# A fused two-layer kernel: the second read of sorted rows in two pieces, and four recurrences moved into later expert slots

## The chip, the cores and the metric

One core of a Trainium2 chip (trn2). The metric is the device time in microseconds, from the launch's start on the device to its end; lower is better. Engines are called by their names or as the profile does: TensorE (PE, its weight loads PEld), VectorE (DVE), ScalarE (ACT), GpSimd (POOL), SyncE (SP).

## The reference, cut to what matters

Eight sequences of 512 tokens with 128 features pass two layers, in float32. Each layer computes `x = x + s * silu(moe(xn))` with `xn = layernorm(x)`. In layer 0, `s` is a gated linear recurrence; in layer 1 it is causal linear attention.

```python
# layer 0, s: per sequence and feature, a scan over the 512 tokens
x_scan = sigmoid(xn @ Wg.T + bg) * tanh(xn @ Wv.T + bv)
a = 0.001 + 0.998 * sigmoid(xn @ Wd.T + bd)
h[t] = a[t] * h[t-1] + x_scan[t]
# layer 0, moe: 4 groups of 2 experts, the best group of a token, both its experts
out = sum_e w[e] * (silu(xn @ gate_w[e]) * (xn @ up_w[e])) @ down_w[e]
```

## The kernel before, in words

**Routing and sorting.** The 32 tiles of 128 tokens are split in two parts of 12 and 20 tiles (`PT`). VectorE computes for each token the row (slot) that it gets in an order sorted by expert group. GpSimd then writes each tile's normalised rows (128 features and 2 expert weights, 520 bytes) to `sorted_rows` in DRAM with one indirect DMA a tile (`scatter`, L422, 32 in all). SyncE reads the sorted rows back (L350 to L352): when part 0's 12 scatters have landed, tiles 0 to 8 (`FULL` = 9 tiles, which part 0 alone fills), and when part 1's 20 have landed, tiles 9 to 34. `sorted_in[h]` counts each read.

**Expert slots.** Layer 0's experts run in `SORTED` = 35 slots, one sorted tile in each. In slot n TensorE (`late_slot`, L934) runs three gate matmuls (L901 to L903), turns the rows of tile n+1 (L926), runs three up matmuls, the eight down matmuls of tile n-2 (L921) and four transposes of the hidden values of tile n-1 (L931). Between them ScalarE does SiLU (L621), the rounding copy of the next rows (`sxT_out`, L616), the copy of the turned hidden values (L625) and of the result (L630). VectorE does the remainder of the next rows (`rest_of_rows`, L1407), without which the next gate can't start, and the product gate x up (L1417). TensorE waits at slot 8 (`FULL - 1`) for `sorted_in[1]`, since slot 8 turns tile 9.

**Recurrences.** Sequence q goes through `rec_project` (three matmuls of 512 columns, L842), `rec_tanh` on ScalarE (decay L564, gate L566, content L567, scaling of the decay L570), `rec_value` (L1336) and `rec_scan` (L1343) on VectorE, `rec_turn` (four transposes, L850) on TensorE and `rec_out` (L575) on ScalarE. The engines' orders are written out by hand and are in-order queues joined by semaphores. Sequences 0 to 4 are scanned before the slots; `LATE` = 3 sequences (5 to 7) have value and scan in slots 0 to 5 and are turned in slots 2, 4, 6 (`TURN_AFTER`). `rec_turn(4)` stands between the up matmuls of slot 0 and the turn of tile 1. All four activations of sequence 7 stand ahead of slot 0's SiLU. Its projection is in banks 3 to 5 of PSUM; gate and up use banks 0 to 3, the turned hidden values bank 4, the down product bank 6, rows bank 7.

**Weights.** Layer 0's expert weights are split in a rounded part (ScalarE, L580) and a remainder (`w_rest`, VectorE, L1349), four groups. Two copies on VectorE (L1401, L1402) hold a fused weight; TensorE waits for them (`fused_out`) before it turns tile 0. After the last `rec_turn` GpSimd splits the layer 1 weights (`split_w13` and others, L438 to L459), since a part of them lies where `scan` lay, and then gathers results (L432) once the first 16 tiles' results are stored.

## Time and profile before

| | |
|---|---|
| median of 3 runs | 391.16 us (390.8 to 391.41) |
| profiled execution | 389.67 us, its span 387.5 us |
| mean granted TensorE clock | 0.982 of 2.4 GHz |
| busy share of the span | TensorE 95%, VectorE 71%, ScalarE 60%, GpSimd 59% |
| chain that ended last | TensorE 77%, ScalarE 8%, GpSimd 4%, DMA 4%, VectorE 4% |
| TensorE's longest wait | 5.2 us, for the read of the sorted rows |

The span runs from the first to the last instruction; the execution's own time has the launch around it as well. A busy share is a mean over very different stages, so the slots are read from the views by time. A line of the timeline is: start, duration, engine, source line, operation, what is written and read, the count, and in brackets how long the engine stood idle before and who ended that.

### The profile page before, as it was taken

The numbers are of one execution on the slowest core, as the hardware profiler recorded it, in microseconds if no ns is written. First come the engines' busy times: TensorE is split into PE (matmuls) and PEld (weight loads), VectorE is DVE, ScalarE is ACT, GpSimd is POOL, SyncE is SP. The second block draws the span as 40 slices with busy tenths as digits, with TensorE's granted clock in tenths as the row PEclk, the third lists the DMA queues.
The fourth block names the chain that finished last, engine by engine and source line by source line (L and its number), as shares of the span: only waits on it lengthen the run. The fifth ranks groups of instructions, "written<-read, shape, count | busy, mean of one in ns | idle before, by whom it ended". The sixth has DMA issues, their size and how long they took to land.

```text
span 387.5 us, 6422 instructions
## 1 busy us (share of the span) xinstructions
PE 368.6 (95%) x1904; PEld 288.7 (74%) x1904; DVE 275.0 (71%) x769; ACT 231.5 (60%) x462; POOL 227.9 (59%) x215
## 2 busy tenths in 40 slices
PE   6999879949999999999999999999999999999996
PEld 5785348938888988876778778778778777786784
DVE  5989957613343547538869889889799799787663
ACT  3777975515545574769675584785675755932312
POOL 4537887690005218207966967977968869267461
PEclk9968999989999999999999999999999999999999
DMA  7997311340013001054240250340600601405100
GB/s 228 270 346 286 92 58 47 108 107 2 0 41 99 28 2 29 0 184 164 69 179 0 68 207 0 112 162 3 255 17 22 253 0 44 203 3 194 51 29 27
DMA packets 26592, 38.66 MB, mean 100 GB/s; under 512 B 2496, under 2 KB 22848, under 8 KB 24128
## 3 DMA queue, kind: packets, MB, share of 16 engines
q1 hardware_dynamic: 24512, 34.03, 26.5%
q0 software_dynamic: 2048, 4.23, 3.4%
q8 instruction: 17, 0.28, 0.3%
q14 instruction: 15, 0.12, 0.1%
HBM read 29.20 MB, written 9.05 MB: 99 GB/s over the span
## 4 chain that ended last, share of the span: by engine, by line
PE 77%; ACT 8%; POOL 4%; DMA 4%; DVE 4%; issue 3%; ACTq 0%; DVEq 0%
PE ps L1072 9%; PE ps L1040 8%; PE ps L1038 8%; PE ps L1039 8%; PE ps L921 6%; PE ps L901 4%; PE ps L842 3%; PE ps L903 3%; PE ps L902 3%; PE ps L1019 3%; PE ps L931 3%; POOL sorted_rows L422 3%; PE ps L990 2%; DMA sorted_sb<-sorted_rows 2%; PE ps L1055 2%
## 5 line engine op out<-in xcount | busy, mean ns | idle before, releaser
L484 POOL TENSOR_TENSOR gu<-gu 128x512 f32<-128x512 f32 x64 | 87.7, 1372 | 52.3 <-DVE gu L1575 48.3
L1038 PE MATMUL ps<-xc_round,w_round 128*128 128x512 f32 (+1 forms) x145 | 74.9, 517 | 0.6 <-DVE gu L1550 0.5
L706 ACT ACTIVATE gu<-gu 128x512 f32<-128x512 f32 x64 | 40.3, 630 | 56.9 <-DVE gu L1575 55.9
L1040 PE MATMUL ps<-xc_round,w_rest 128*128 128x512 f32 (+1 forms) x145 | 57.1, 394 | 0.0
L1039 PE MATMUL ps<-xc_rest,w_round 128*128 128x512 f32 (+1 forms) x145 | 56.7, 391 | 0.0
L432 POOL DMA_INDIRECT xnT<-sorted_y,slot x32 | 31.7, 990 | 38.6 <-DMA sorted_y<-sorted_sb 32.2
L1575 DVE TENSOR_TENSOR gu<-ps,w_raw 128x512 f32<-128x512 f32 x64 | 43.6, 686 | 11.7 <-PE ps L1040 9.7
L1407 DVE TENSOR_TENSOR sx_rest<-ps,sx_round 128x128 fp32r<-128x128 f32 x35 | 10.2, 291 | 57.6 <-ACT sx_round L616 57.6
L625 ACT COPY h0T<-ps 128x512 f32<-128x512 f32 x35 | 20.5, 587 | 43.7 <-PE ps L931 43.7
L1072 PE MATMUL ps<-gu,w2s 128*128 128x512 f32 x90 | 46.0, 593 | 0.0
L422 POOL DMA_INDIRECT sorted_rows<-sorted_sb,slot x32 | 36.2, 1130 | 14.8 <-issue 9.4
L901 PE MATMUL ps<-w_round,sx_round 128*128 x70 | 34.5, 493 | 7.8 <-DMA sorted_sb<-sorted_rows 5.2
L921 PEld LDWEIGHTS ps<-w0d,h0T 128*128 128x128 f32 x280 | 37.2, 193 | 3.2
L921 PE MATMUL ps<-w0d,h0T 128*128 x280 | 37.3, 276 | 0.0
L1038 PEld LDWEIGHTS ps<-xc_round,w_round 128*128 128x128 f32 x145 | 27.4, 189 | 11.7 <-issue 7.6
L1039 PEld LDWEIGHTS ps<-xc_rest,w_round 128*128 128x128 f32 x145 | 27.5, 190 | 10.2 <-issue 7.7
L1417 DVE SCALAR_TENSOR_TENSOR h<-sg,sorted_sb,ps 128x256 f32<-128x256 f32 x70 | 30.2, 473 | 3.3 <-PE ps L931 2.6
L1040 PEld LDWEIGHTS ps<-xc_round,w_rest 128*128 128x128 f32 x145 | 27.2, 188 | 6.1
L903 PE MATMUL ps<-w_rest,sx_round 128*128 x70 | 28.1, 402 | 0.0
L902 PE MATMUL ps<-w_round,sx_rest 128*128 x70 | 28.1, 401 | 0.0
L1575 DVE TENSOR_TENSOR gu<-ps,w0d 128x512 f32<-128x512 f32 x32 | 21.6, 683 | 7.6 <-PE ps L1040 7.5
L621 ACT ACTIVATE sg<-ps 128x512 f32<-128x512 f32 x35 | 21.0, 599 | 10.0 <-PE ps L903 10.0
(230 smaller groups left out, 831.2 us busy)
## 6 DMA issues: line engine op xcount, KB each, us to landing
w_raw<-score_rows SPq DMA_DIRECT2D x8, 1024.0 KB, 5.9
spread_first<-score_rows SPq DMA_DIRECT2D x4, 1024.0 KB, 4.9
w0d<-score_rows SPq DMA_DIRECT2D x4, 1024.0 KB, 7.1
sorted_rows<-zero_rows SPq DMA_DIRECT2D x1, 2340.0 KB, 15.7
xa<-in_x SPq DMA_DIRECT2D x8, 256.0 KB, 4.5
w_raw<-in_gate_up SPq DMA_DIRECT2D x1, 2048.0 KB, 13.9
out_x<-xa SPq DMA_DIRECT2D x7, 256.0 KB, 2.2
sorted_sb<-sorted_rows SPq DMA_DIRECT2D x1, 1690.0 KB, 9.0
```

What stands on the lines that cost most here:

```text
L422: pool.indirect_dma_start(sorted_rows, bass.IndirectOffsetOnAxis(ap=slot[:, t:t + 1], axis=0), rows[:, t, :], None).then_inc(scattered[h], 16)
L484: pool.tensor_tensor(gu[:, e % RING, 1, :], gu[:, e % RING, 0, :], gu[:, e % RING, 1, :], ALU.mult).then_inc(s["m_h"], 1)
L706: nc.scalar.activation(gu[:, e % RING, 0, :], gu[:, e % RING, 0, :], ACT.Silu).then_inc(s["m_sg"], 1)
L901: pe.matmul(bank, sx_round[:, par, :], w0_round[:, c], start=True, stop=False)
L902: pe.matmul(bank, sx_rest[:, par, :], w0_round[:, c], start=False, stop=False)
L903: return pe.matmul(bank, sx_round[:, par, :], w0_rest[:, c], start=False, stop=True)
L921: last = pe.matmul(ps[:, bank, 0:P], h0T[:, par, c * P:(c + 1) * P], w0d[:, bass.ds(g + c * P, P)], start=(c == 0), stop=(c == HC - 1))
L1038: pe.matmul(bank, w13_round[:, c], xc_round[par][:, some], start=True, stop=False)
L1039: pe.matmul(bank, w13_round[:, c], xc_rest[par][:, some], start=False, stop=False)
L1040: pe.matmul(bank, w13_rest[:, c], xc_round[par][:, some], start=False, stop=True).then_inc(s["m_gu"], 1)
L1072: pe.matmul(ps[:, 3, :], w2s[:, w * P:(w + 1) * P], gu[:, e % RING, 1, :], start=(e == 0), stop=(e == E1)).then_inc(s["m_y"], 1)
L1575: nc.vector.tensor_tensor(gu[:, p % RING, part, :], ps[:, BANKS[u % RING], :], spread[j % 2][(e - 1) // (E1 // 2)][:, c:c + SEQ], ALU.mult ...
```

## The change

1. `ROWS_FROM`: the read of tiles 9 to 34 becomes two, of tiles 9 to 11 and 12 to 34, issued one after the other. TensorE waits for the first at slot 8 and for the second at slot 11; VectorE waits for the second at slot 12.
2. `LATE` becomes 4: sequences 4 to 7 have value and scan in slots 5 to 12, and sequences 3 to 7 are turned and copied out in slots 5, 7, 9, 11 and 13. The two last loops of `w_rest` come ahead of the fused copies on VectorE.
3. Sequence 7 is projected into banks 4 to 6. Only its gate activation stands ahead of slot 0; decay, content and scaling come in slots 0, 1 and 2. TensorE waits for them one by one (slots 1, 2 and 5), by the new semaphore `rec_gated` and by two old ones.
4. A fourth set of buffers (`gy`, `xn1`, `s1`), used later in layer 1, holds sequence 7 until its scan.
5. ScalarE's rounding copy of tile 0 comes right behind the activations of sequence 6.

```diff
+ROWS_FROM = (0, FULL, FULL + 3, SORTED)
-LATE = 3
-TURN_AFTER = (2, 4, 6)
+LATE = 4
+LATE_FROM = 5
+TURN_AFTER = tuple(LATE_FROM + 2 * i for i in range(LATE + 1))
-REC_BANKS = (SEQS - LATE) * (6,) + LATE * (5,)
+REC_BANKS = (SEQS - LATE - 1) * (6,) + (LATE + 1) * (5,)
...
+        rec_set = (0, 1, 2, 0, 1, 2, 0, 3)
+
+        def rec_bank(q, i):
+            return 3 * (q % 2) + i if q < SEQS - 1 else 4 + i
...
-            for h, n in enumerate((slice(0, FULL), slice(FULL, SORTED))):
+            for piece, (first, stop) in enumerate(zip(ROWS_FROM, ROWS_FROM[1:])):
+                h = min(piece, PARTS - 1)
                 sp.wait_ge(scattered[h], 16 * PT[h])
-                sp.dma_start(sorted_sb[:, n, :], rows_t[:, n, :]).then_inc(sorted_in[h], 16)
+                sp.dma_start(sorted_sb[:, first:stop, :], rows_t[:, first:stop, :]).then_inc(sorted_in[piece], 16)
...
# ScalarE
-            for q in range(4, SEQS - 1):
-                rec_tanh(q)
-                rec_out(q - 3)
...
+            for q in range(4, SEQS - 1):
+                rec_tanh(q)
+                if q == SEQS - 2:
+                    sxT_out(0, 0)
+                if q < SEQS - LATE + 2:
+                    rec_out(q - 3)
...
-            sxT_out(0, 0)
-            rec_tanh(SEQS - 1)
-            rec_out(SEQS - LATE - 1)
+            act.wait_ge(s["rec_mm"], SEQS)
+            rec_gate(SEQS - 1)
             for n in range(SORTED):
                 late_slot(n)
-                for i in range(LATE):
+                if n == 0:
+                    rec_decay(SEQS - 1)
+                if n == 1:
+                    rec_content(SEQS - 1)
+                if n == 2:
+                    rec_scale(SEQS - 1)
+                for i in range(LATE + 1):
                     if n == TURN_AFTER[i]:
-                        rec_out(SEQS - LATE + i)
+                        rec_out(SEQS - LATE - 1 + i)
...
# TensorE
                 wait(pe, "rec_act", q - 1)
+                if q == SEQS - 1:
+                    pe.wait_ge(s["rec_out"], SEQS - LATE - 1)
...
             for q in range(4, SEQS - 1):
                 rec_project(q)
-                rec_turn(q - 3)
+                if q < SEQS - LATE + 2:
+                    rec_turn(q - 3)
...
-            rec_turn(SEQS - LATE - 1)
...
                 if n == FULL - 1:
                     pe.wait_ge(s["group_ready"], PARTS)
-                    pe.wait_ge(sorted_in[1], 16)
+                if n + 1 in ROWS_FROM[1:-1]:
+                    pe.wait_ge(sorted_in[ROWS_FROM.index(n + 1)], 16)
...
                 if n == 1:
                     pe.wait_ge(s["down0_in"], 16)
+                    pe.wait_ge(s["rec_gated"], SEQS)
+                if n == 2:
+                    pe.wait_ge(s["rec_keep"], 2 * SEQS - 1)
+                if n == TURN_AFTER[0]:
                     pe.wait_ge(s["rec_act"], SEQS)
-                    pe.wait_ge(s["rec_out"], SEQS - LATE)
                 late_slot(n)
-                for i in range(LATE):
+                for i in range(LATE + 1):
                     if n == TURN_AFTER[i]:
-                        rec_turn(SEQS - LATE + i)
+                        rec_turn(SEQS - LATE - 1 + i)
...
# VectorE
-                if n == FULL:
-                    dve.wait_ge(sorted_in[1], 16)
+                if n in ROWS_FROM[1:-1]:
+                    dve.wait_ge(sorted_in[ROWS_FROM.index(n)], 16)
                 late_slot(n)
-                if n == 2 * LATE:
+                if n == FULL - 3:
                     groups_of_tiles(FULL, SORTED, steps[0:1, :], step_by[:, :])
                 for i in range(LATE):
-                    if n == 2 * i:
+                    if n == LATE_FROM + 2 * i:
                         rec_value(SEQS - LATE + i)
-                    if n == 2 * i + 1:
+                    if n == LATE_FROM + 2 * i + 1:
                         rec_scan(SEQS - LATE + i)
```

## Rows read from the trace of the kernel before

**Rows 1.** The page, part 1: TensorE's busy time, share of the span, instructions.
```profile
PE 368.6 (95%) x1904; PEld 288.7 (74%) x1904; DVE 275.0 (71%) x769; ACT 231.5 (60%) x462; POOL 227.9 (59%) x215
```

**Rows 2.** The chain that ended last, 70 to 88 us: start, duration, what.
```profile
71.39 2.29 DMA sorted_rows<-sorted_sb,slot
...
73.69 8.96 DMA sorted_sb<-sorted_rows
...
82.97 0.65 PE ps L901
```

**Rows 3.** TensorE's timeline: eighth projection, gates of slots 0 to 3, 7, 9, 10.
```profile
49.94 2.74 PE L842 MATMUL ps<-xnT,a0w 128*128 128x512 f32 x6
53.17 0.49 PE L901 MATMUL ps<-w_round,sx_round 128*128 x1 [0.49 <-DVE sx_rest L1407]
...
57.00 0.49 PE L901 MATMUL ps<-w_round,sx_round 128*128 x1 [1.64 <-DVE sx_rest L1407]
...
59.22 0.49 PE L901 MATMUL ps<-w_round,sx_round 128*128 x1
...
62.50 0.47 PE L901 MATMUL ps<-w_round,sx_round 128*128 x1
...
74.72 0.47 PE L901 MATMUL ps<-w_round,sx_round 128*128 x1
...
87.40 0.47 PE L901 MATMUL ps<-w_round,sx_round 128*128 x1
...
90.23 0.48 PE L901 MATMUL ps<-w_round,sx_round 128*128 x1
```

**Rows 4.** Windows, TensorE alone: stretch, length, busy (instructions), granted clock, DMA share, GB/s.
```profile
82.97:87.40 4.43, 4.43 (x19) 0.61 0.00 0
```

**Rows 5.** DMA issues: what, queue, count, KB each, us from issue to landing.
```profile
sorted_sb<-sorted_rows SPq DMA_DIRECT2D x1, 1690.0 KB, 9.0
...
sorted_sb<-sorted_rows SPq DMA_DIRECT2D x1, 585.0 KB, 4.2
```

**Rows 6.** The timeline of all engines, 48 to 51 us: a scan and two scatters.
```profile
48.18 1.23 DVE L1343 TENSOR_TENSOR_SCAN scan<-td,tg 128x512 f32<-128x512 f32 x1
...
48.41 1.75 POOL L422 DMA_INDIRECT sorted_rows<-sorted_sb,slot  x1 [0.30 <-issue]
...
50.47 2.01 POOL L422 DMA_INDIRECT sorted_rows<-sorted_sb,slot  x1 [0.30 <-issue]
```

**Rows 7.** VectorE's timeline: weight remainders, second fused copy, next rows, groups of tiles.
```profile
45.93 1.22 DVE L1349 TENSOR_TENSOR w_rest<-w_raw,w_round 128x1024 fp32r<-128x1024 f32 x1
...
47.27 0.27 DVE L1402 COPY bv_wo<-ps 128x128 f32<-128x128 f32 x1
...
49.32 2.33 DVE L1349 TENSOR_TENSOR w_rest<-w_raw,w_round 128x1024 fp32r<-128x1024 f32 x2
...
56.57 0.29 DVE L1407 TENSOR_TENSOR sx_rest<-ps,sx_round 128x128 fp32r<-128x128 f32 x1 [3.54 <-ACT sx_round L616]
...
75.62 0.17 DVE L1331 CAST group<-group_f 1x26 int32<-1x26 f32 x1
```

**Rows 8.** Groups by line, 53 to 99 us: busy us, mean ns, idle before.
```profile
L422 POOL DMA_INDIRECT sorted_rows<-sorted_sb,slot x15 | 15.3, 1020 | 4.6 <-issue 4.6
```

**Rows 9.** ScalarE's timeline, 51 to 59 us.
```profile
51.88 0.59 ACT L575 COPY sT<-ps 128x512 f32<-128x512 f32 x1
...
52.72 0.69 ACT L564 ACTIVATE td<-ps,a0bh 128x512 f32<-128x512 f32 x1
...
56.26 0.27 ACT L616 CAST sx_round<-ps 128x128 fp32r<-128x128 f32 x1
58.00 0.60 ACT L621 ACTIVATE sg<-ps 128x512 f32<-128x512 f32 x1 [1.46 <-PE ps L903]
```

**Rows 10.** GpSimd's timeline: the first weight split and the first gather.
```profile
75.04 0.61 POOL L438 CAST w_round<-w_raw 128x512 fp32r<-128x512 f32 x1 [2.69 <-PE ps L850]
...
119.25 1.00 POOL L432 DMA_INDIRECT xnT<-sorted_y,slot  x1 [32.17 <-DMA sorted_y<-sorted_sb]
```

More of the change, by code:

```diff
@@ L241, in gated_recurrent_moe_two_layers @@
             [("w13_round", [P, W13S], F32R), ("of", [P, SEQ], F32)])
-        rec_d, rec_g, rec_v = (td[:, 0, :], td[:, 1, :], gf[:, :]), (tg[:, 0, :], tg[:, 1, :], qT[:, :]), (tv[:, 0, :], tv[:, 1, :], kT[:, :])
+        rec_d = (td[:, 0, :], td[:, 1, :], gf[:, :], gy[:, :])
+        rec_g = (tg[:, 0, :], tg[:, 1, :], qT[:, :], xn1[:, :, :].rearrange("p t d -> p (t d)"))
+        rec_v = (tv[:, 0, :], tv[:, 1, :], kT[:, :], s1[:, :, :].rearrange("p t d -> p (t d)"))
+        rec_set = (0, 1, 2, 0, 1, 2, 0, 3)
+        def rec_bank(q, i):
+            return 3 * (q % 2) + i if q < SEQS - 1 else 4 + i
         h0, h0T, gu = in_one_place(
@@ L271, in gated_recurrent_moe_two_layers @@
             counted placed tot_out slots_ready group_ready bias0_ready bias1_ready
-            rec_mm rec_act rec_keep rec_x rec_scan rec_turned rec_out fused fused_out
+            rec_mm rec_gated rec_act rec_keep rec_x rec_scan rec_turned rec_out fused fused_out
             w0_rounded w0_split f_turned f_xT f_xr f_gate f_up f_sg f_h f_hT f_hTs f_down f_y
@@ L278, in gated_recurrent_moe_two_layers @@
         x_in = [sem(f"x_in{q}") for q in range(SEQS)]
-        sorted_in = [sem(f"sorted_in{h}") for h in range(PARTS)]
+        sorted_in = [sem(f"sorted_in{piece}") for piece in range(len(ROWS_FROM) - 1)]
         y_stored = [sem(f"y_stored{h}") for h in range(PARTS)]
@@ L560, in rec_tanh, with rec_decay, rec_gate, rec_content @@
             def rec_tanh(q):
-                par, to = q % 2, q % 3
                 act.wait_ge(s["rec_mm"], q + 1)
                 wait(act, "rec_scan", q - 2)
-                nc.scalar.activation(rec_d[to], ps[:, 3 * par + 2, :], ACT.Tanh, bias=a0bh[:, 2:3],
-                                     scale=0.5).then_inc(s["rec_keep"], 1)
-                nc.scalar.activation(rec_g[to], ps[:, 3 * par, :], ACT.Tanh, bias=a0bh[:, 0:1], scale=0.5)
-                nc.scalar.activation(rec_v[to], ps[:, 3 * par + 1, :], ACT.Tanh,
+                rec_decay(q)
+                rec_gate(q)
+                rec_content(q)
+                rec_scale(q)
+            def rec_decay(q):
+                nc.scalar.activation(rec_d[rec_set[q]], ps[:, rec_bank(q, 2), :], ACT.Tanh, bias=a0bh[:, 2:3],
+                                     scale=0.5).then_inc(s["rec_keep"], 1)
+            def rec_gate(q):
+                nc.scalar.activation(rec_g[rec_set[q]], ps[:, rec_bank(q, 0), :], ACT.Tanh, bias=a0bh[:, 0:1],
+                                     scale=0.5).then_inc(s["rec_gated"], 1)
+            def rec_content(q):
+                nc.scalar.activation(rec_v[rec_set[q]], ps[:, rec_bank(q, 1), :], ACT.Tanh,
                                      bias=a0b[:, 1:2]).then_inc(s["rec_act"], 1)
+            def rec_scale(q):
+                to = rec_set[q]
                 act.wait_ge(s["rec_keep"], 2 * q + 1)
@@ L838, in rec_project @@
             def rec_project(q):
-                par = q % 2
                 wait(pe, "rec_act", q - 1)
+                if q == SEQS - 1:
+                    pe.wait_ge(s["rec_out"], SEQS - LATE - 1)
                 for i in (2, 0, 1):
-                    last = pe.matmul(ps[:, 3 * par + i, :], a0w[:, i * P:(i + 1) * P],
+                    last = pe.matmul(ps[:, rec_bank(q, i), :], a0w[:, i * P:(i + 1) * P],
                                      xnT[:, q * SEQ:(q + 1) * SEQ], start=True, stop=True)
@@ L1333, in rec_value @@
             def rec_value(q):
-                to = q % 3
+                to = rec_set[q]
                 dve.wait_ge(s["rec_act"], q + 1)
@@ L1338, in rec_scan @@
             def rec_scan(q):
-                to = q % 3
+                to = rec_set[q]
                 dve.wait_ge(s["rec_x"], q + 1)
```

## Prediction, made before the changed kernel was run

> **What bounds the kernel now.** I read four views in this order: the page's busy shares, the chain that ended last, TensorE's instructions in order of time, and the windows with their granted clock. The reader should see that TensorE is busy for 95% of the span [rows 1], so nearly everything that leaves its queue is time saved, and that the one large hole is in the expert slots of layer 0. The chain runs through the last of the 32 scatters (71.39 to 73.69), the read of the 26 tiles of part 1 (73.69 to 82.65) and then slot 8's first matmul at 82.97 [rows 2]. Slots follow each other at 2.83 us (90.23 minus 87.40), and at 3.28 us where four transposes of a recurrence (`rec_turn`) sit in them (62.50 minus 59.22), so one `rec_turn` costs 0.45 us [rows 3]. Slot 7 began at 74.72 and slot 8 was due at 77.55, so it came 5.42 us late. Slot 8 then lasted 4.43 us (82.97 to 87.40), 1.60 us over a usual one, because the granted clock in it was 0.61 (a mean over a stretch at 1.2 GHz and one at 2.4 GHz) after 5 us without matmuls [rows 4]; slot 9 has its 2.83 us again [rows 3]. Together the late read costs 7.02 us.
>
> I call the start of slot n's first gate matmul G(n). In the slots TensorE's queue sets the pace, apart from the start: before G(1) = 57.00 it stood idle for 1.64 us, waiting for VectorE's remainder of the next rows [rows 3].
>
> **Edit 1, part 1 in two pieces.** Slot 8 now waits only for tiles 9 to 11, slot 11 for tiles 12 to 34. The read of 26 tiles (1690 KB) took 9.0 us and that of 9 tiles (585 KB) 4.2 us [rows 5]. The line through both is 0.28 us a tile, so 3 tiles (195 KB) take 4.2 - 6 x 0.28 = 2.5 us. The bounds are 2.3 us (a scatter's landing, the smallest transfer here [rows 2]) and 4.2 us. I take 2.5, since two reads of the same form give it. Edit 1 adds one issue of SyncE (0.4 us) and nothing waits behind it but the second piece, which then lands about 0.4 to 1.3 us later than the whole read did.
>
> The Trainium skill speaks against cutting a transfer: "DMA: Bandwidth & Descriptors", section Anatomy of one DMA, gives about 2.0 us fixed for each one (for transfers that GpSimd issues). By its formula piece one would take 2.0 + 0.2 / 0.436 = 2.5 us, an estimate that equals the line above, and the second fixed cost would lie beside the data; what the cut costs is only paid if slot 11 waits.
>
> **Edit 2, when the read can start.** It starts when all 20 scatters of part 1 have landed, so the scatter queue on GpSimd counts. A scatter takes 0.96 us, with 0.30 us of issue between two. Some take longer: the one at 48.41 lasted 1.75 while a scan ran on VectorE from 48.18 to 49.41, and the one at 50.47 lasted 2.01 [rows 6] while `w_rest` ran until 51.65 [rows 7]. Each ends about 0.8 us after that VectorE instruction does, as if it had been held until just before its end. All held ones began inside a `rec_value`, `rec_scan` or `w_rest`, whose two inputs lie in SBUF. From 53 us on 15 scatters took 15.3 us [rows 8] where 15 x 0.96 = 14.4: 0.9 us of holding, beside `rec_value` and `rec_scan` of sequences 5 to 7. These VectorE instructions move to slots 5 to 12, behind the scatters. Before them, `rec_value(4)` and `rec_scan(4)` leave and the `w_rest` instructions close up to 45.93 to 49.40; of the scatters at 47.15, 48.41 and 50.47 only one is then held, for 0.9 us instead of 0.8 + 1.05. So the last scatter starts 0.9 + 0.9 = 1.8 us sooner, at 69.6, and the read is issued at 71.9. Bounds: no gain (73.7) and 1.8.
>
> The skill's page "SBUF — State Buffer", section Who interferes with whom, says that a two-input VectorE operation holds only GpSimd's reads, and infers that it does not hold descriptor generation. By it the scatters would not move; the rows above (1.75 and 2.01 against 0.96) speak against it. Its result is rival 2.
>
> Piece one then lands at 71.9 + 2.5 = 74.4 and is seen 0.3 us later [rows 2], at 74.7; piece two at 71.9 + 9.0 + 0.4 + 0.3 = 81.6 (bound 73.7 + 9.0 + 1.3 + 0.3 = 84.3).
>
> **Edit 3, the start.** On ScalarE, `rec_out(3)` (0.59 us at 51.88) goes, and the four activations of sequence 7, which kept it busy from 52.72 on and pushed the copy for tile 1 to 56.26 [rows 9], are spread over slots 0 to 2; one, the gate, stays ahead of slot 0. On VectorE the three last `w_rest` now precede the fused copies. 3 x 1.17 us from 45.93 give 49.40, and the two copies (0.27 us each, 0.2 apart) end at 49.85 instead of 47.54 [rows 7]. TensorE needs them before it turns tile 0: it does so at 50.05, the eighth projection follows at 50.15 (now 49.94) and takes 2.7 us, and gate 0 follows that at 52.8 (now 53.17) [rows 3]. Gate and up take 1.42, tile 1 is turned by 54.5. ScalarE does the eighth gate's tanh at 52.9 to 53.6, slot 0's SiLU 1.0 us after G(0) as in slot 1 [rows 9], at 53.8, and the copy for tile 1 at 54.55. From that copy to the gate there are 0.74 us now (56.26 to 57.00), so G(1) = 55.3: **1.7 us gained**. Bounds: 0.4 (only gate 0's gain) and 2.1 (ScalarE not in the way at all).
>
> The new TensorE waits are met: gates read at 53.6 (needed for slot 1), decay read at 55.4 (needed for slot 2 at 57.5), content at 58.7 (needed for slot 5). The content and the 0.7 us scaling on ScalarE fall in slots 1 to 3; the copy for tile 4 then starts at 62.37 and G(4) needs it by 62.45, so this costs nothing but has only 0.1 us of slack. If that cover is gone, a tenth or two of a us.
>
> **Edit 4, the turns.** Before slot 8 stood three `rec_turn` in slots, and `rec_turn(4)` ahead of slot 1 lay in the idle 1.64 us. Now five are in slots 5, 7, 9, 11, 13: two more, **0.9 us lost**. `rec_turn(3)` also lay ahead of slot 0.
>
> **Edit 5, VectorE in slot 6.** There `groups_of_tiles` (it ended at 75.8, which is G(6) = 74.72 - 3.28 = 71.44 plus 4.3 [rows 7]) is now followed by `rec_scan(4)`, 1.22 us. G(6) becomes 55.3 + 2.22 + 4 x 2.83 + 0.45 = 69.3, so the scan ends at 74.9, where `sx_rest` of slot 8 starts; gate matmuls start 0.43 us after it (56.57 to 57.00), at 75.35. G(8) by TensorE's own queue is 69.3 + 2.83 + 2.83 + 0.45 = 75.4. So VectorE is just in time; I charge 0.1 us. Piece one (74.7) is earlier. Slot 8 starts at 75.5 at full clock and the clock loss goes too. What is late next is nothing: slot 11 is due at 75.5 + 2.83 + 3.28 + 2.83 = 84.4 against 81.6 for piece two.
>
> **Edit 6, GpSimd's later start.** `split_w13` waits for the last `rec_turn`, now in slot 13 (about 93.5) instead of slot 6. GpSimd starts at 94.2 instead of 75.04; its 12 us of splits end at 106.3. Its next work, the gathers, began at 119.25 after 32.17 us of idling [rows 10] and will be due near 111.5. So it is hidden, with 5 us to spare. All behind follows the slots unchanged. The change of buffers (`gy`, `xn1`, `s1`) costs nothing: their next users come in slot 23 or later.
>
> **The sum.** G(9) was 87.40 and becomes 75.5 + 2.83 = 78.3, 9.1 us sooner; the three turns in slots 9, 11, 13 give back 1.35. Written as terms: 5.42 (hole) + 1.60 (clock) + 1.7 (start) - 0.9 (turns) - 0.1 = **7.7 us**. The profiled execution took 389.67 us with a span of 387.5; it should become 382.0 and 379.8. The median of the three timed runs is 391.16, 1.5 above the profiled one; I take the saving off the median: **383.5 us**.
>
> **The rivals.** (1) The start gains nothing or little, because another wait (the new position of the fused copies, the eighth projection's two waits) takes its place. Then G(8) is due at 77.1, piece one is surely there, and 5.42 + 1.60 - 0.9 = 6.1 us remain: 385.0. For it: project, turn and copy are a tight chain of 0.2 us slacks; against it: each row of it is known. 13%. (2) The scatters do not come sooner (the skill's rule above): piece one is seen at 73.7 + 2.5 + 0.3 = 76.5 instead of 75.4, price 1.1: 384.5. 13%. (3) The small read takes as long as the 9 tile one and starts at 73.7: seen at 78.2, a wait of 2.8 us and perhaps 1.6 of clock: gain 5.0 to 3.4, 386.2 to 387.8. 7%. (4) Slot 11 waits for piece two, up to 1 us: 384.5. 4%. (5) The other side: the two pieces share queues and engines, their packets mix, and both land when all bytes are there. Then slot 8 starts at 82.97 + 0.4 after a hole of 8 us, runs at the low clock again (G(9) = 87.8), and the three turns behind it are added: 0.4 + 1.35 = 1.75 us slower, 392.9 (with the scatters sooner, 391.1). It decides from a landing of piece one at about 81.3 (87.40 - 1.35 - 4.43 - 0.3). Against it: the first piece is issued 0.4 us ahead on one queue, and it has a ninth of the bytes. 5%, of which 3 slower and 2 the same.
>
> **How the numbers follow.** The forecast of 383.5 has 58%. The range reaches from 382.7 (no VectorE charge, start at its upper bound) to 386.0, which holds cases 1, 2 and 4 and leaves out 3 and 5 with the tails. Less than 0.2% (0.8 us, about what a measurement of this kernel can tell from no change) has 2%, slower 3%, faster 95%.
>
> **What would show it.** Right: no TensorE wait for a read before slot 8 or 11, granted clock 1.00 from 53 us on, G(1) near 55.3, G(8) near 75.5, G(14) 7.7 us before its 101.6 of now (87.40 + 5 x 2.83), scatters of 0.96 us from 50 us on, the last at 69.6, the first piece landing in 2.5 us. Wrong: an idle time ahead of slot 8 (releaser DMA: case 2 or 3; VectorE: edit 5), G(1) later than 56, longer slots 2 to 4 (ScalarE), or a clock below 1 in them.

## The result and the profile after

| | before | after |
|---|---|---|
| median of 4 runs | 391.11 us (390.8 to 391.41) | 384.53 us (380.98 to 387.52) |
| profiled execution | 389.67 us, span 387.5 | 380.98 us, span 378.9 |
| mean granted clock of it | 0.982 | 0.986 |

The ratio is 0.9758 [0.9726, 0.9789], or 9.5 us saved, and by it the time is 381.6 us; it compares the two lower runs of the changed kernel (380.98 and 382.29), since the two others (386.78 and 387.52) lie over 1.5% above the lowest. Against the forecast of 383.5 (382.7 to 386.0) the median of all four is 1.0 us above, and the time by the ratio is 1.9 us below and outside the range. The forecast was wrong by that, although nearly every step of its sum came true in the trace. Between the two profiled executions the change saved 8.7 us (389.67 to 380.98), where 7.7 were forecast. In later jobs on other chips the saving was smaller, and in some it was none.

The profiled execution went as follows. First the page of the changed kernel: its head, TensorE's row, the granted clock in 40 slices, and the chain that ended last.

```profile
span 378.9 us, 6424 instructions
...
PE 366.4 (97%) x1904; PEld 287.3 (76%) x1904; DVE 275.7 (73%) x769; ACT 231.1 (61%) x462; POOL 226.3 (60%) x215
...
PEclk9968999999999999999999999999999999999999
...
PE 80%; DVE 12%; ACT 4%; issue 2%; POOL 1%; DMA 1%; ACTq 0%
```

TensorE was busy for 2.2 us less than in [rows 1] in a span that is 8.6 us shorter: what went was idle time and 1.6 us that the low clock had cost. DMA has all but left the chain (4% before, 1% now). Next, TensorE's timeline of the changed kernel: tile 0's turn, the eighth projection, and the first gate of slots 0, 1, 7, 8, 9 and 14 (the second gate of each slot and the rest left out).

```profile
49.59 0.33 PE L958 MATMUL ps<-cst,sorted_sb 128*128 128x128 f32 x1 [0.42 <-DVE bv_wo L1437]
49.75 2.75 PE L873 MATMUL ps<-xnT,a0w 128*128 128x512 f32 x6
52.34 0.50 PE L933 MATMUL ps<-w_round,sx_round 128*128 x1
...
54.88 0.49 PE L933 MATMUL ps<-w_round,sx_round 128*128 x1 [0.77 <-DVE sx_rest L1442]
...
71.77 0.48 PE L933 MATMUL ps<-w_round,sx_round 128*128 x1
...
75.03 0.48 PE L933 MATMUL ps<-w_round,sx_round 128*128 x1
...
77.88 0.48 PE L933 MATMUL ps<-w_round,sx_round 128*128 x1
...
93.35 0.48 PE L933 MATMUL ps<-w_round,sx_round 128*128 x1
```

In the whole timeline no gate from slot 2 to slot 14 waits for anything. Slot 8 follows slot 7 after 3.26 us (a slot of 2.83 with a turn of 0.45), where it came after 8.25 us in [rows 3]; slot 8 lasts 2.85 us in place of 4.43. The same stretch on SyncE, GpSimd and VectorE, the changed kernel again:

```profile
46.87 1.96 POOL L431 DMA_INDIRECT sorted_rows<-sorted_sb,slot  x1 [0.30 <-issue]
...
69.33 0.95 POOL L431 DMA_INDIRECT sorted_rows<-sorted_sb,slot  x1 [0.30 <-issue]
...
71.62 0.91 SPq L361 DMA_DIRECT2D sorted_sb<-sorted_rows  x2
...
73.24 1.23 DVE L1378 TENSOR_TENSOR_SCAN scan<-td,tg 128x512 f32<-128x512 f32 x1
74.39 0.26 DVE L1442 TENSOR_TENSOR sx_rest<-ps,sx_round 128x128 fp32r<-128x128 f32 x1
...
93.66 0.61 POOL L447 CAST w_round<-w_raw 128x512 fp32r<-128x512 f32 x1 [23.38 <-PE ps L881]
...
111.00 1.00 POOL L441 DMA_INDIRECT xnT<-sorted_y,slot  x1 [5.21 <-DMA sorted_y<-sorted_sb]
```

The last scatter starts at 69.33 and both pieces are issued from 71.62 on (whole read at 73.69 in [rows 2]). The DMA issues of the changed kernel, with size and time to landing, give what the pieces took:

```profile
sorted_sb<-sorted_rows SPq DMA_DIRECT2D x1, 1495.0 KB, 8.9
...
sorted_sb<-sorted_rows SPq DMA_DIRECT2D x1, 195.0 KB, 2.7
```

Piece one, 195 KB, has landed by 74.3, before slot 8 asks for it at 75.03; piece two by about 81, where slot 11 starts at 83.98.

**The sum against the two traces.** Between the kernels, everything up to TensorE's turn at 46 us was 0.33 us earlier already (46.29 and 45.96), which is no part of the change. The rest of the distance between G(14) = 101.57 before and 93.35 after:

| stretch | before | after | gained | forecast |
|---|---|---|---|---|
| up to G(1), less the 0.33 | 56.67 | 54.88 | 1.79 | 1.7 |
| G(1) to G(7) | 17.72 | 16.89 | 0.83 | 0.9 (two turns fewer here) |
| G(7) to G(9) | 12.68 | 6.11 | 6.57 | 5.42 + 1.60 - 0.45 - 0.1 |
| G(9) to G(14) | 14.17 | 15.47 | -1.30 | -1.35 |
| sum | | | 7.89 | 7.7 |

Behind it 0.27 us more came at slot 26, whose gate waited 0.38 us for VectorE before and not at all now, and 0.1 behind slot 34. (Every kernel below that reads part 1 in one piece has this wait at slot 26, 0.35 to 0.38 us, and none that reads it in two pieces has it; why isn't known.) With the 0.33 that makes the 8.6 us between the spans.

### The profile page after: what moved, and what is told of

Its sections match the earlier page's. It is cut to its first block, busy times and chain, and to the rows that moved or that the text cites. A ratio compares the mean times of both kernels' runs of the same rounds, so it can differ in the third digit from the quotient of the medians.

```text
span 378.9 us, 6424 instructions
## 1 busy us (share of the span) xinstructions
PE 366.4 (97%) x1904; PEld 287.3 (76%) x1904; DVE 275.7 (73%) x769; ACT 231.1 (61%) x462; POOL 226.3 (60%) x215
## 4 chain that ended last, share of the span: by engine, by line
PE 80%; DVE 12%; ACT 4%; issue 2%; POOL 1%; DMA 1%; ACTq 0%
PE ps L1104 10%; PE ps L1072 8%; PE ps L1070 8%; PE ps L1071 8%; PE ps L953 8%; PE ps L933 5%; PE ps L935 4%; PE ps L934 4%; PE ps L963 4%; PE ps L1051 3%; PE ps L1022 2%; PE ps L1087 2%; PE ps L990 2%; DVE st L1254 2%; DVE w_rest L1384 1%
## 5 line engine op out<-in xcount | busy, mean ns | idle before, releaser
L1442 DVE TENSOR_TENSOR sx_rest<-ps,sx_round 128x128 fp32r<-128x128 f32 x35 | 10.2, 290 | 50.5 <-ACT sx_round L634 50.4
L431 POOL DMA_INDIRECT sorted_rows<-sorted_sb,slot x32 | 34.4, 1075 | 14.8 <-issue 9.4
L873 PE MATMUL ps<-xnT,a0w 128*128 128x512 f32 x48 | 24.4, 652 | 0.0
```

The costliest lines, as they stand in the source:

```text
L431: pool.indirect_dma_start(sorted_rows, bass.IndirectOffsetOnAxis(ap=slot[:, t:t + 1], axis=0), rows[:, t, :], None).then_inc(scattered[h], 16)
```

## The experiments

In what follows, *the changed kernel* and *the kernel before* are the two unaltered ones. Each job ran on one chip, with runs of the kernel before between the others, and each chip had one job, so a chip and its moment can't be told apart. In three jobs (the first comparison's, chips 9 and 5) the kernel before took 386.9 to 392.5 us; in four (chips 0, 7, 4 and 13) it took 394 to 414, with standstills that the last section of this part shows.

### Which part brought what

**The read undone.** Of the whole change only the cut of the read is taken back.

```diff
-ROWS_FROM = (0, FULL, FULL + 3, SORTED)
+ROWS_FROM = (0, FULL, SORTED)
```

> The changed kernel with part 1 read in one piece of 26 tiles (edit 1 undone, all else kept). My theory: the read starts at 71.6 us and takes 9.0, so slot 8 starts at about 80.9 instead of 75.0 and runs at the low clock: 5.9 + 1.6 = 7.5 us over the changed kernel, 388.5 us, 1.1 to 2.5 below the kernel before. Rival (the pieces are worth little, since the moved recurrences brought the gain): within 2 us of the changed kernel.

Measured: 389.66 us (389.08 to 390.3, 10 runs), ratio 0.9988 [0.9964, 1.0012]. By the ratio all but 0.5 us is gone, which can't be told from nothing; by medians it is 1.0 us (390.61 beside it), where at least 1.1 was expected. TensorE's timeline of this kernel, the first gates of slots 7, 8 and 9:

```profile
72.20 0.48 PE L933 MATMUL ps<-w_round,sx_round 128*128 x1
...
80.71 0.79 PE L933 MATMUL ps<-w_round,sx_round 128*128 x1 [5.00 <-DMA sorted_sb<-sorted_rows]
...
86.06 0.78 PE L933 MATMUL ps<-w_round,sx_round 128*128 x1
```

The start gained (G(1) = 55.32) and the read was issued at 71.75, 1.9 us sooner than in the kernel before, which confirms edit 2; but the hole stayed at 80.71 - 72.20 - 3.28 = 5.23 us, and at the low clock slot 8 lasted 5.35 us in place of 2.83 and slot 9 0.29 too long. The low clock cost 2.8 us here (2.52 + 0.29), against 1.60 in the profile of the kernel before; so the 1.60 of the forecast is one execution's. G(14) was 101.88, 0.3 us later than in the kernel before. So the 1.7 us of the start only made TensorE wait longer, and the three turns behind the hole ate most of what the earlier read gave. The moved recurrences and the earlier start alone are worth next to nothing.

**The read alone.** The kernel before with only the pieces and their waits.

```diff
+ROWS_FROM = (0, FULL, FULL + 3, SORTED)
...
+                if n + 1 in ROWS_FROM[1:-1]:
+                    pe.wait_ge(sorted_in[ROWS_FROM.index(n + 1)], 16)
```

> The kernel before with the read in two pieces alone. My theory: the read starts at 73.7, the 3 tiles land 2.7 us later and are seen at 76.7, before slot 8 is due at 77.55; hole and low clock go, 5.4 + 1.6 = 7.0 us, so 382.7 for the profiled execution (before 389.7). Rival (the pieces alone are not enough because the scatters end too late): a wait of over 0.5 us ahead of slot 8 and a gain under 6 us.

Measured: 383.97 us (382.31 to 386.04, 4 runs), ratio 0.9827 [0.9782, 0.9871]. The whole change, on the same chip, gave 385.53 us and 0.9871 [0.9828, 0.9913]: the times can't tell the one-line change from the whole. Its first gates of slots 7, 8 and 9:

```profile
77.40 0.47 PE L903 MATMUL ps<-w_round,sx_round 128*128 x1
...
80.23 0.48 PE L903 MATMUL ps<-w_round,sx_round 128*128 x1
...
83.07 0.48 PE L903 MATMUL ps<-w_round,sx_round 128*128 x1
```

G(7) to G(9) takes 5.67 us where it took 12.68: the cut alone gives 7.01 us, the 5.42 + 1.60 of the prediction to a hundredth. (This profiled execution took 385.17 us where 382.7 was expected: its start, G(0), was 2.65 us later, with a granted clock of 0.50 from 12 to 16 us; more on that below.) The pieces were issued at 73.85, as late as the whole read had been, and piece one took 2.7 us: seen at 76.9, it would have been in time for slot 8 of the kernel before too, due at 77.55. From G(0) to G(34) this kernel takes 102.18 us, the changed kernel 101.72 and the kernel before 109.39. So of the 7.7 us between G(0) and G(34) the cut alone has 7.2. The other edits add 0.5 there and 0.5 ahead of G(0) (0.83 less the 0.33), by these profiles.

**The recurrences three slots earlier.**

```diff
-LATE_FROM = 5
+LATE_FROM = 2
```

> The changed kernel with values, scans and turns of the late recurrences from slot 2 on (turns at 2, 4, 6, 8, 10). My theory of the scatters: each scatter that begins inside a value or scan of VectorE is held until just before that instruction's end; two to four of those from 60 us on now last 1.1 to 1.9 us instead of 0.96, the last one starts 0.4 to 1.2 us later than at 69.33, and piece one is seen by 75.5. Slot 8 is due 0.45 us later than in the changed kernel (three turns ahead of it instead of two), the sum of turns is the same: total within 0.4 us of the changed kernel. Rival (a scatter is longer for another reason, for instance the DMA traffic early in the kernel): all scatters from 53 us on at 0.96 us.

Measured: 385.26 us (384.34 to 386.54), ratio 0.9877 [0.9843, 0.9911], beside 385.53 for the changed kernel on the same chip: no difference. The last scatter starts at 69.51, where 0.4 to 1.2 us behind 69.33 was expected, and from 60 us on one scatter is held and not two to four. A view of GpSimd's and VectorE's timelines of this kernel shows what holds a scatter:

```profile
63.16 0.74 DVE L1371 SCALAR_TENSOR_TENSOR tg<-tg,tv 128x512 f32<-128x512 f32 x1
...
63.18 0.96 POOL L431 DMA_INDIRECT sorted_rows<-sorted_sb,slot  x1 [0.30 <-issue]
...
66.98 0.96 POOL L431 DMA_INDIRECT sorted_rows<-sorted_sb,slot  x1 [0.31 <-issue]
...
67.05 1.22 DVE L1378 TENSOR_TENSOR_SCAN scan<-td,tg 128x512 f32<-128x512 f32 x1
...
69.27 0.68 DVE L1371 SCALAR_TENSOR_TENSOR qT<-qT,kT 128x512 f32<-128x512 f32 x1
...
69.51 1.28 POOL L431 DMA_INDIRECT sorted_rows<-sorted_sb,slot  x1 [0.30 <-issue]
```

The scatter at 69.51 starts 0.24 us into a `rec_value` and is held until after its end at 69.95. The one at 66.98 has started before the scan and isn't held. The one at 63.18, 0.02 us behind the start of a `rec_value`, isn't held either; here it is VectorE's instruction that takes 0.74 in place of 0.68 us. Two others, at 43.38 and 45.22 us, began well inside a scan and 0.04 us behind the start of a `rec_value`, and took 1.54 and 1.48. So a scatter pays only when it begins inside such an instruction and neither at its very start nor at its very end, and with other phases most of them pay nothing. This kernel also showed a wait that nobody had expected: 1.55 us of TensorE before slot 2, for ScalarE's content activation (`s`, L586), since the wait that stands at the first turn slot moved from slot 5 to slot 2. Moving a constant moved a wait with it.

### Where the spread comes from

**The changed kernel twice more**, unaltered, on chips 9 and 5.

> The changed kernel unaltered, timed again. The four runs so far took 381.0 and 382.3 us at a mean granted clock of 0.986 and 0.982, and 386.8 and 387.5 us at 0.969 and 0.966. Theory A (the kernel has two levels: in some executions TensorE's clock falls to 1.2 GHz in one more stretch): runs again in two groups some 5 us apart, the longer ones at a clock near 0.967. Theory B (those two runs were disturbed from outside): all runs within 1.5 us, clock near 0.984, while the kernel before would be disturbed as often.

> The changed kernel once more, beside its filled version on one chip. Theory C: its time follows the mean granted clock of the run, about 381.5 us at 0.986 and 387 at 0.968, since TensorE has no idle time left that could absorb a low stretch. On a chip where engines also stand for 2 to 5 us without a releaser in the profile (as in the last session, where all kernels took 394 to 408 us), it is as slow as the kernel before plus or minus 2.

| job | before: median, lowest to highest | changed: median, lowest to highest | ratio |
|---|---|---|---|
| first | 391.11, 390.8 to 391.41 | 384.53, 380.98 to 387.52 | 0.9758 [0.9726, 0.9789] |
| chip 9 | 390.61, 387.11 to 391.71 | 385.53, 381.98 to 387.41 | 0.9871 [0.9828, 0.9913] |
| chip 5 | 390.41, 386.9 to 392.47 | 384.14, 382.09 to 385.19 | 0.9837 [0.9806, 0.9869] |

Median against median the change saves 6.6, 5.1 and 6.3 us. The execution's time follows the mean granted clock, if loosely: on chip 9 the changed kernel took 381.98 and 382.02 us at 0.985 and 0.987, and 385.33, 385.72, 386.68 and 387.41 at 0.971, 0.975, 0.973 and 0.969. The windows with TensorE's clock show where it differs. Stretch, length, busy (instructions), granted clock, DMA share, GB/s; first the changed kernel in the first profile (380.98 us), then on chip 5 (385.19 us):

```profile
8.00:21.00 13.00, 11.39 (x76) 1.00 1.12 283
21.00:33.00 12.00, 12.00 (x44) 0.57 1.02 399
33.00:50.00 17.00, 14.96 (x47) 1.00 0.36 115
```
```profile
8.00:21.00 13.00, 12.08 (x56) 0.74 1.12 281
21.00:33.00 12.00, 11.96 (x55) 0.57 1.02 394
33.00:50.00 17.00, 15.49 (x44) 0.90 0.37 120
```

Both run most of 21 to 33 us at the lower of the two clock levels. On chip 5 the clock had fallen once already between 12 and 20 us, where TensorE comes from routing matmuls (128x12) and turns of tiles, and it stayed low 3.4 us longer after 33 us; by the three rows the lower level lasted 10.2 us longer in all. The first `rec_project` took 5.47 us in place of 2.82:

```profile
13.66 5.47 PE L873 MATMUL ps<-xnT,a0w 128*128 128x512 f32 x6
```
```profile
12.82 2.82 PE L873 MATMUL ps<-xnT,a0w 128*128 128x512 f32 x6
```

(chip 5 first, then the first profile.) G(0) came at 56.50 instead of 52.34, G(34) at 158.20 instead of 154.06: the 4.16 us of a late start arrive as 4.14 at the end. From G(0) to G(34) the two profiles differ by 0.02 us. So these two executions differ by their start alone; that the whole spread of the changed kernel's times (6.5 us in the first job) comes from it is likely, as the clocks follow, but only these profiles show where.

The times don't show plainly that the hole keeps a kernel steadier. For it: the kernel with one read, which has the hole, stayed within 1.2 us in 10 runs on chip 9, where the changed kernel spread over 5.4 us in 6. Against it: the kernel before has the hole too, and spread over 4.6 us there, and over 5.6 us on chip 5, where the changed kernel spread over 3.1.

In one profile, that of chip 9, piece one took 3.7 us instead of 2.7, and TensorE waited 0.5 us for it; the forecast had 0.7 us of slack there.

**Filling the gaps.** Six zero matmuls of 256 columns stand among the routing matmuls, and four more of 260 columns ahead of the first turn; in the changed kernel and in the kernel before.

```diff
-WARM = 8
+WARM = 12
+FILL = 1
...
+            def fill(bank=4):
+                for i in range(FILL):
+                    pe.matmul(ps[:, bank, 2 * P:4 * P], zero_rows[:, 0:P], zero_rows[:, 0:2 * P], start=True, stop=True)
...
             route(3)
+            fill()
```

> The changed kernel with 12 warm-up matmuls and six matmuls of zeros. In the last session the stretch at 1.2 GHz from 21 to 32 us was gone in its profile, but engines stood still elsewhere. Theory C on a quiet chip: 377 to 380 us, clock 0.99 or more, spread under 3 us; the fill is worth 2 to 4 us beside the changed kernel. If the low stretch was not worth 5.1 us because ScalarE and VectorE set the pace up to 50 us: within 1 us of the changed kernel's better runs.

> The kernel before with the same fill. Theory C on a quiet chip: only what reaches the scatters is saved, 388 to 390 us. Rival: it saves as much as in the changed kernel, 386 to 388, which would mean that the hole at slot 8 absorbs nothing.

Measured on chip 5: the changed kernel with it 383.71 us (380.53 to 384.74), ratio 0.9821 [0.9785, 0.9857], at clocks of 0.991 to 1.0, 0.4 us below the changed kernel beside it, which can't be told from nothing; the kernel before with it 390.39 us, ratio 1.0002 [0.9976, 1.0029]. Both fell short of what was expected (377 to 380 us, and 388 to 390). The window of 21 to 33 us is at full clock now:

```profile
21.00:33.00 12.00, 11.68 (x70) 1.00 1.02 394
```

and it gives nearly nothing, since TensorE now waits for VectorE behind it: 1.70 us before 42.30 and 2.30 us before 50.92. Behind the second wait the clock fell again in this profile, and the eighth projection took 4.38 us in place of 2.75. TensorE's longest waits in this kernel (who waits, for whom: us in total, times, longest):

```profile
PE ps L970 <- DVE bv_wo L1449: 2.3, 1, 2.3
PE ps L882 <- DVE scan L1390: 1.7, 1, 1.7
PE ps L848 <- DVE sorted_sb L1402: 1.2, 1, 1.2
```

The two executions at a clock of 1.0 took 380.53 and 382.03 us, no less than unfilled ones at 0.985 to 0.987 (380.98 to 382.46). So the low clock of 21 to 33 us, which all unaltered profiles of these three jobs have, costs little, because VectorE's own chain lies beside it (12% of the chain of the changed kernel). What makes the clock fall at 10 to 20 us in some executions of one kernel and not in others stays open.

The same on chip 0, with `WARM = 2` and with two zero matmuls in each place as well, says nothing about the fill:

> The changed kernel with 2 instead of 8 warm-up matmuls at the start (they multiply zeros; the result is untouched). Theory C (the spread of the changed kernel's runs, 381 to 387.5 us, is TensorE at 1.2 GHz in one or two more stretches before 35 us, and without the hole at slot 8 nothing absorbs that): the clock is low over most of 1 to 18 us in every run, each us of it costs half a us where TensorE is dense, mean clock 0.97 or less, 385 to 388 us, no run below 384. Rival D (the spread comes from later, for instance the DMA queues): still spread between 381 and 387.5.

> The changed kernel with 12 warm-up matmuls and six further matmuls of zeros (256 columns, 0.44 us each at 2.4 GHz) between the turns and routing products of 15 to 27 us, where the clock fell at 21 us in every profile so far. Theory C: if they keep the clock up, the stretch of 10.2 us at 1.2 GHz (21 to 31 us) goes, worth up to 5.1 us less about 1.5 us for the added matmuls that no idle time covers: 377 to 379 us, mean clock 0.99 and over, and runs closer together. If the clock still falls: 382 to 384 and the same spread as before. Rival D: no change of the spread in either case.

> As fill1 with two matmuls of zeros in each of the six places (5.3 us in all, some 1.1 us of it in idle time). Theory C: the clock stays up more surely, the cost is 2.6 us more than fill1 wherever fill1 holds it too: 379 to 381 with runs within 1 us of each other.

> The kernel before with the same 12 warm-up matmuls and six matmuls of zeros as fill1. Theory C: the routing and the scatters start up to 2 us sooner if the clock holds, and the read with them, since slot 8 waits for the scatters and not for TensorE: 388 to 390 us, 1 to 2 us saved, less than in the changed kernel.

The changed kernel took 404.42 us with `WARM = 2`, 403.5 with one zero matmul in each place and 403.95 with two, the kernel before with one 400.86, and unaltered 401.2 us (394.14 to 408.32). That chip had another trouble.

### Jobs with a standstill

Does the kernel before absorb a late start of TensorE in its hole, while the changed one passes it on? A kernel of each kind issues the eighth projection twice, which delays TensorE by 2.75 us and leaves VectorE, the scatters and the reads alone.

```diff
-                for i in (2, 0, 1):
+                for i in (2, 0, 1) * (2 if q == SEQS - 1 else 1):
```

> The changed kernel with the three matmuls of the eighth projection issued twice, so that TensorE reaches slot 0 later by one projection (2.75 us in its trace) while VectorE, the scatters and the reads are left alone. Theory (without the hole a late start of TensorE passes in full to the end): slots 0 to 34 all 2.7 us later, no wait for a read, time 2.7 us above the unaltered changed kernel beside it, at equal granted clock. Rival (some later wait of the slots absorbs it, such as the one of 0.8 us before slot 1, or slot 26's): 2.0 us or less.

> The kernel before with the eighth projection issued twice in the same way (2.74 us). Theory (the hole before slot 8 absorbs a late start, since the read's end hangs on the scatters and not on TensorE): slot 7 starts 2.7 us later, slot 8 at the same 83.0, the wait for the read falls from 5.2 to about 2.5 us; the time stays within 0.3 us of the kernel before, or falls by up to 1.6 us if the clock no longer falls after the shorter hole. Rival (the scatters and the read move with the slots' VectorE work): the time rises by 1 to 2.7 us.

> The changed kernel unaltered, as the base of the two runs with a doubled projection. Theory (its time varies with the granted clock of the first 35 us and passes that on in full): again between 381 and 387.5 us, with runs of equal mean clock within 0.7 us of each other; median 5 to 7 us below the kernel before. Rival (the first look's 380.98 was typical and the later ones disturbed): a median below 382.5.

Medians on chip 7: kernel before 401.17 us (396.23 to 414.34, 29 runs), changed 402.22, ratio 1.0053 [1.0021, 1.0085]; doubled projection 403.57 (changed) and 401.88 (before). The additions of 1.35 and 0.71 us for the doubled projection decide nothing here: every time is 10 us or more above what was expected, and in the profiles of the changed kernel G(0) came sooner with the doubled projection (54.99) than without it (57.60). In this job **the changed kernel is slower than the kernel before**, by 0.5%. TensorE's timeline of the unaltered changed kernel there, the first gate of slot 2, the down matmuls of slot 2, the gates of slots 3 and 4, and beside it ScalarE's instructions:

```profile
62.35 0.49 PE L933 MATMUL ps<-w_round,sx_round 128*128 x1
...
66.38 0.58 ACT L650 COPY h0T<-ps 128x512 f32<-128x512 f32 x1 [4.50 <-remote]
...
67.10 2.07 PE L953 MATMUL ps<-w0d,h0T 128*128 x8 [2.99 <-ACT h0T L650]
...
70.62 0.60 ACT L646 ACTIVATE sg<-ps 128x512 f32<-128x512 f32 x1 [3.07 <-remote]
...
72.73 0.27 ACT L634 CAST sx_round<-ps 128x128 fp32r<-128x128 f32 x1 [1.51 <-remote]
...
73.47 0.65 PE L933 MATMUL ps<-w_round,sx_round 128*128 x1 [3.44 <-issue]
...
77.89 0.48 PE L933 MATMUL ps<-w_round,sx_round 128*128 x1
```

ScalarE stands for 4.50, 3.07 and 1.51 us, with a releaser ("remote") that occurs in none of the profiles of the three faster jobs, and TensorE with it. Slot 2 lasts 11.12 us. A second such stop follows in slot 22 (131.16 to 138.97). GpSimd isn't touched: its scatters go on at 0.96 us each, and each stop lies around the end of a train of indirect DMAs (the last scatter started at 70.00, the eighth gather at 134.99). Now the kernel before with the doubled projection on the same chip, the first gates of slots 4, 7 and 8:

```profile
76.68 0.49 PE L901 MATMUL ps<-w_round,sx_round 128*128 x1
...
86.07 0.47 PE L901 MATMUL ps<-w_round,sx_round 128*128 x1
...
88.91 0.48 PE L901 MATMUL ps<-w_round,sx_round 128*128 x1
```

Slot 8 follows slot 7 after 2.84 us: there is no hole. TensorE has lost over 6 us between G(0) and G(4) (18.41 us against 12.16), the scatters have not, and the whole read, issued at 73.56 and landed in 8.2 us, is there by 82. In both kernels slot 4 begins where the stop ends (77.89 and 76.68, with G(0) at 57.60 and 58.27). What then remains of the change is its cost: from G(4) to G(22) the changed kernel takes 53.27 us and this one 51.99, a difference of 1.28 where three turns more are 1.35.

> The changed kernel unaltered, base of the two. Without the standstill: 5 to 9 us below the kernel before. With it: the read has landed before TensorE reaches slot 8 in either kernel, so nothing of the 7.0 us is to be had and the three additional turns behind slot 7 are lost: 1 to 2 us above the kernel before.

> The changed kernel with the eighth projection issued twice, once more, for a chip on which TensorE does not stand still near 65 and 135 us. Theory (a late start of TensorE passes in full to the end): 2.7 us above the unaltered changed kernel beside it. Rival (later waits absorb it): 2.0 us or less. If TensorE and ScalarE do stand still near 65 us as in the run before, the theory expects slot 4 near 77 us whatever the start, and 0 to 1.5 us.

> The kernel before with the eighth projection issued twice, once more. Theory (the hole before slot 8 absorbs the late start): slot 8 at the same time as in the kernel before, the wait for the read 2.5 us, the time within 0.3 us of it or lower by up to 1.6 us (clock). Rival: 1 to 2.7 us above. With the standstill near 65 us: slots 4 to 34 take 1.35 us less than in the changed kernel, three turns of 0.45.

Chip 4 repeated it. Kernel before 402.07 us (399.15 to 405.95), changed 403.33, ratio 1.003 [0.9998, 1.0062]; doubled 404.85 and 403.23. G(4) was 77.69 and 78.09, and from G(4) to G(22) 53.28 us stood against 52.00. The changed kernel's 1.26 us above is inside what was expected with a standstill, though the interval just reaches 1. The kernel before with the doubled projection on chip 13, where engines stand still too:

> The kernel before with the eighth projection issued twice (2.74 us), a third time, its base being the kernel before beside it. Without the standstill, theory (the hole before slot 8 absorbs a late start): slot 7 2.7 us later, slot 8 at about 83, the wait for the read 2.5 us in place of 5.2, the time within 0.3 us of the kernel before or lower by up to 1.6 us, if the clock no longer falls after the shorter hole. Rival (the scatters and the read move with the start of the slots): 1 to 2.7 us above. With the standstill near 65 us (time about 400 us): no wait for the read, and nothing is told apart.

404.56 us beside 402.4, ratio 1.0054 [1.0015, 1.0092]. So the doubled projection was never timed without the standstill. But two profiles of one kernel answer the question. The kernel before with the fill ran on chips 5 and 0, and on chip 0 one standstill of ScalarE (2.51 us) fell ahead of slot 5. The first gates of slots 7 and 8, chip 5 first:

```profile
74.77 0.47 PE L913 MATMUL ps<-w_round,sx_round 128*128 x1
...
83.00 0.79 PE L913 MATMUL ps<-w_round,sx_round 128*128 x1 [5.15 <-DMA sorted_sb<-sorted_rows]
```
```profile
77.11 0.48 PE L913 MATMUL ps<-w_round,sx_round 128*128 x1
...
83.14 0.79 PE L913 MATMUL ps<-w_round,sx_round 128*128 x1 [2.94 <-DMA sorted_sb<-sorted_rows]
```

Slot 7 is 2.34 us later, slot 8 0.14 us and slot 10 0.06 us (91.50 and 91.56): the hole swallows lost time of TensorE. For time lost before the slots the scatters tell how far the read would move too. In the profile with the read alone G(0) was 2.65 us later than in the kernel before and the last scatter 0.16 us (71.55 and 71.39). Between the two profiles of the changed kernel G(0) differs by 4.16 us and the issue of the read by 1.03 us (72.65 and 71.62), so a hole would have taken some 3 us of the 4.16, by estimate.

## Why the prediction was right in its steps and wrong in its time

**The hole and the clock** (5.42 + 1.60): right. The read alone gave 7.01, and taking the cut back brought the hole (5.23 us) and the low clock back, which then cost 2.8 us and not 1.60.

**Edit 1:** 2.5 us were forecast for piece one from the line through two rows, and 2.7 measured (up to 3.7 in other profiles, inside the bounds of 2.3 to 4.2). The second piece landed at about 81 against 81.6. The Trainium skill ("DMA: Bandwidth & Descriptors", Anatomy of one DMA) gives, for transfers that GpSimd issues, a fixed part of 2.0 us and the bytes over 436 GB/s; by it piece one would take 2.5 us, an estimate, near the 2.7. That SyncE's reads follow it isn't shown: for 1495 KB the same formula gives 5.5 us, an estimate, and the trace 8.9. What the cut costs was not paid, as slot 11 had 3 us to spare.

**Edit 2:** 69.6 was forecast for the last scatter and 69.33 measured, or 69.66 without the 0.33 us that were there before. From 45.6 us on one scatter was held (1.96 us at 46.87) and all others took 0.95 or 0.96. Rival 2 did not happen. It rested on an inference of the Trainium skill ("SBUF — State Buffer", Who interferes with whom), that VectorE operations with two SBUF inputs leave descriptor generation alone. The traces show that they hold an indirect DMA's instruction on GpSimd: 1.96 us with `w_rest` on VectorE, 1.28 us inside a `rec_value`, 0.96 otherwise. That need not contradict the inference: by the same section such operations do hold a GpSimd instruction that reads SBUF, and a scatter reads its row numbers (`slot`) there. Which of the two is held no run shows; "the scatters would not move" didn't follow from the page. The size for one was right (0.9 forecast, 1.00 measured), but as the run with recurrences from slot 2 shows, moving them out of the way is a matter of phase, and the cut made it unneeded: with the read alone, issued at 73.85, piece one was in time.

**Edit 3, start:** 1.7 forecast, 1.79 measured. The wait before G(1) fell to 0.77 and names `sx_rest`, as before. Tile 0's turn came at 49.59, 0.46 sooner than forecast (0.13 without the 0.33), as the fused copies ended sooner.

**Edit 4, turns:** 0.9 forecast; 0.83 - 1.30 - 0.45 = -0.92 measured over the three stretches.

**Edit 5:** the scan of slot 6 was to end at 74.9 and `sx_rest` to follow; it started at 74.39, before the scan's modelled end at 74.47. Slot 8 came 3.26 us behind slot 7, so the charge of 0.1 was not needed.

**Edit 6:** GpSimd started its splits at 93.66 (forecast 94.2), ended them at 105.79, and waited 5.21 us for the gathers' data: hidden with the 5 us that were foreseen.

**What failed** is the last step, "I take the saving off the median", with the range around it, which held bounds for the steps and nothing for the execution as a whole. The ratio's saving is 9.5 us (391.11 to 381.64, the mean of the two lower runs), 1.8 more than the 7.7 forecast. Of these 1.8 us, 0.3 is what that execution was ahead by at 46 us already, 0.2 lies in the steps up to G(14), 0.4 behind G(14) (slot 26's wait, which was never looked at, and 0.1 behind slot 34) and 0.1 outside the span. The last 0.8 come from the step itself: the kernel before stands in the ratio with its median, 1.44 us above its profiled execution, and the changed kernel with two runs that lie 0.66 us above its own. The prediction took those 1.5 us for a constant of the kernel. They go with the execution: the kernel before took 388.7 to 389.9 us at a clock of 0.982 on chip 9 and 390.6 to 391.7 at 0.969, and the profile shown had 0.982. What the slower executions of the kernel before did differently stays open, as no profile of one was kept. The range's lower end doesn't follow from the two reasons given for it either: no VectorE charge and a start of 2.1 us give 382.9, not 382.7.

That the time fell below the range and not into it is in part the luck of which executions were drawn. By the ratios of chips 9 and 5 the time is 385.6 and 384.0 us, inside the range, and the saving 5.0 and 6.4 us, under the forecast.

Another thing was missing from the prediction. It doesn't explain the miss above, but it decides what the change is worth: the hole was a buffer. With it TensorE's lost time upstream of slot 8 was in large part free; without it that time is paid. The saving is 8.6 us between two profiles with good starts, 5 to 6.6 us by medians in three jobs, and the change costs 1.1 and 1.3 us in the two jobs with the standstill where the unaltered kernels ran side by side. The rival "slower than before" was a mechanism that did not happen (pieces landing together); the one that did happen needs no fault in the change: something else stops TensorE before slot 8 for longer than the read is late.

## What to carry to other kernels

When an engine waits for a transfer, cut the transfer so that its first use gets a small piece: here 7 us for one line, which in the times can't be told from the whole change, where moving work to start the whole read 1.9 us sooner gave almost nothing. Before counting a removed hole as saved, ask what else stops the same engine upstream and how much that varies: a hole absorbs it, and the saving is what remains in the executions where nothing does. And forecast a range for the execution too, from the spread of the runs of before and their granted clocks, not from the terms alone.

## What the runs showed of the hardware that was not expected

- In four of seven jobs (chips 0, 7, 4 and 13) ScalarE stood still, for up to 7.6 us at a time between 58 and 76 us and for 5.1 to 6.2 us in one piece between 124 and 139 us, in every profile of these jobs, of changed kernels or not, with the releaser "remote", and TensorE with it. Around these times a train of indirect DMAs of GpSimd (32 scatters, 8 gathers) came to its end. The kernel before took 394 to 414 us there in place of 387 to 392. Why isn't known, nor whether it belongs to the chip or to the moment.
- An indirect DMA's 0.96 us on GpSimd becomes 1.28 to 2.01 when it begins well inside a VectorE instruction with two inputs in SBUF (`rec_value`, `rec_scan`, `w_rest`), 1.13 when 0.36 us of that instruction are left, and stays at 0.96 when it begins before it or when 0.16 us or less are left; one that began 0.02 us after its start took 0.96 too, and VectorE's own instruction then 0.74 instead of 0.68 us.
- Two profiles of one kernel, on two chips, differ by 10.2 us at the 1.2 GHz level within their first 40 us, and their times by 4.2 us (380.98 and 385.19). With zero matmuls between the small ones of the routing the clock stayed full from 21 to 33 us, and the time was the same within what the runs can tell (0.4 us less by medians), as TensorE then waited for VectorE.
- The same read of 195 KB took 2.7 to 2.9 us in ten profiles, 3.1 us in one, and 3.6 and 3.7 us in two.
